# Feed-forward products of a cross-attention kernel as three fp32r matmuls on high and low parts

## The reference

```python
qn = layernorm(x, ln_q_g, ln_q_b);  q = qn @ Wq * scale
k, v = split(media @ Wkv)                            # 16 heads of 64
attn = softmax(where(mask, q k^T, -inf));  x = x + tanh(attn_gate) * (attn v) @ Wo
h = layernorm(x, ln_ff_g, ln_ff_b)
x = x + tanh(ff_gate) * gelu(h @ W1, exact) @ W2     # W1 256 x 1024, W2 1024 x 256
# second layer, on x:
mem = media @ W_mem^T;  ctx = softmax(x mem^T / 16) mem
gate = sigmoid([x, ctx] @ W_gate^T + b_gate);  out = rmsnorm(x + gate * ctx) * norm_w
```

## Time and profile before

| | us |
|---|---|
| median of 3 runs (lowest, highest) | 870.41 (870.37, 870.51) |
| profiled execution | 869.72 |
| span in its trace, first to last instruction | 867.9 |
| PE busy in the span | 831.4 |
| DVE, ACT, POOL busy | 591.0, 465.6, 401.2 |

### The profile page before, as it was taken

The page is one execution under the profiler, slowest core; times in us unless marked ns, Lnnn a source line. Parts: engine busy times, 40 slices in busy tenths (PEclk is TensorE's granted clock), DMA queues, the critical chain, the costliest instruction groups (busy, mean ns, idle before and its releaser), DMA issues.

```text
span 867.9 us, 18230 instructions
## 1 busy us (share of the span) xinstructions
PE 831.4 (96%) x7777; PEld 698.4 (80%) x7777; DVE 591.0 (68%) x968; ACT 465.6 (54%) x727; POOL 401.2 (46%) x189
## 2 busy tenths in 40 slices
PE   4999999999999999999999999999999999998986
PEld 3788888888888888888888888888888778887775
DVE  7856788867577888675688886756788622126375
ACT  5755666657356666573566665635555441226352
POOL 2445565655625656556256565553566650000002
PEclk9999999999999999999999999999999999999999
DMA  9100001000000010000000000000000700000201
GB/s 283 26 1 2 2 5 37 1 2 2 2 1 2 10 32 1 2 2 2 2 1 2 2 1 2 2 2 2 1 2 4 214 1 1 1 1 1 77 1 48
DMA packets 20559, 16.80 MB, mean 19 GB/s; under 512 B 1008, under 2 KB 19456, under 8 KB 20480
## 3 DMA queue, kind: packets, MB, share of 16 engines
q1 hardware_dynamic: 20192, 15.38, 6.0%
q10 hardware_dynamic: 288, 0.27, 0.1%
HBM read 14.59 MB, written 1.05 MB: 18 GB/s over the span
## 4 chain that ended last, share of the span: by engine, by line
PE 81%; DVE 11%; ACT 4%; POOL 2%; issue 1%; DMA 1%; ACTq 0%; POOLq 0%; DVEq 0%
PE psum L1284 21%; PE psum L1298 17%; PE psum L345 15%; PE psum L1253 6%; PE psum L1209 4%; PE psum L1313 3%; PE psum L1060 3%; PE psum L1074 3%; PE psum L1148 2%; DVE mx L901 2%; DVE ot L931 1%; DVE k_lo L890 1%; PE psum L1304 1%; ACT v L614 1%; POOL acc L450 1%
## 5 line engine op out<-in xcount | busy, mean ns | idle before, releaser
L450 POOL TENSOR_TENSOR acc<-acc,ring 128x1024 f32<-128x1024 f32 x128 | 306.8, 2397 | 18.7 <-POOL acc L445 0.5
L901 DVE TENSOR_REDUCE mx<-psum 128x2 f32<-128x800 f32 (+2 forms) x256 | 245.2, 989 | 84.5 <-PE psum L1253 72.4
L631 ACT ACTIVATE ring<-psum 128x1024 f32<-128x1024 f32 x192 | 197.0, 1027 | 65.7 <-PE psum L1284 59.2
L445 POOL TENSOR_TENSOR acc<-ring 128x1024 f32<-128x1024 f32 x32 | 77.0, 2405 | 271.6 <-ACT ring L631 271.6
L1298 PE MATMUL psum<-ring,v 128*64 128x256 f32 (+1 forms) x1664 | 186.7, 381 | 1.8
L1298 PEld LDWEIGHTS psum<-ring,v 128*64 128x64 f32 (+1 forms) x1664 | 116.7, 137 | 61.1 <-DVE k_lo L890 3.9
L1284 PE MATMUL psum<-nm,maskrow 64*128 64x256 f32 (+1 forms) x832 | 123.9, 294 | 0.6 <-ACT ring L631 0.6
L1284 PE MATMUL psum<-q_lo,k_hi 64*128 64x256 f32 (+1 forms) x832 | 116.9, 278 | 0.0
L1284 PE MATMUL psum<-q_hi,k_hi 64*128 64x256 f32 (+1 forms) x832 | 116.7, 277 | 0.0
L1284 PE MATMUL psum<-q_hi,k_lo 64*128 64x256 f32 (+1 forms) x832 | 116.5, 277 | 0.0
L623 ACT COPY od<-psum 128x512 f32<-128x512 f32 x32 | 18.8, 588 | 161.0 <-PE psum L1304 161.0
(11 more groups left out here) (150 smaller groups left out, 1352.9 us busy)
## 6 DMA issues: line engine op xcount, KB each, us to landing
nat<-in_ctx_dram SPq DMA_DIRECT2D x7, 768.0 KB
w<-in_L_xattn_W_dram SPq DMA_DIRECT2D x2, 1024.0 KB, 8.7
wo<-in_L_xattn_Wo_dram SPq DMA_DIRECT2D x1, 1024.0 KB, 9.7
out_dram<-t_res SPq DMA_DIRECT2D x8, 128.0 KB, 1.7
mask<-in_mask_BxS_bk_dram SPq DMA_DIRECT2D x4, 200.1 KB, 7.1
nat<-in_ctx_dram SPq DMA_DIRECT2D x2, 384.0 KB, 7.4
ring<-in_L_xattn_Wkv_dram SPq DMA_DIRECT2D x2, 384.0 KB, 6.2
wq<-in_L_xattn_Wq_dram SPq DMA_DIRECT2D x1, 768.0 KB, 6.7
```

What stands on the lines that cost most here:

```text
L445: nc.gpsimd.tensor_tensor(acc[:, :, :, :], ring[:, 0, :, :, :], ring[:, 1, :, :, :], ALU.add)\
L450: nc.gpsimd.tensor_tensor(acc[:, :, :, :], acc[:, :, :, :], ring[:, g, :, :, :], ALU.add)\
L631: nc.scalar.activation(ring[:, g, :, :, :], score_set[m % 2].rearrange("p (h i q) -> p h i q", h=2, i=2), ACT.Exp).then_inc(S["p_ready"], 1)
L901: nc.vector.tensor_reduce(mx[:, t, :, c], pair[:, :, 0:min(c1, KEYS) - c0], axis=AX.X, op=ALU.max).then_inc(S["m_max"], 1)
```

## The change

The feed-forward products get the form that the projections have. `hidden` and `ff_out` do three fp32r matmuls for each float32 one. Four things supply the parts:

- POOL splits W1 in four pieces of 128x512, two behind pair 3 and two behind pair 4 of the last batch (each a cast and a subtraction), and W2 likewise behind pairs 6 and 7 (`split_ff_weights`). It first waits for the DVE fold of that pair (`acc_ready`).
- DVE splits the tokens (`split_tokens`, item `d.i`, 128x512) and the GELU's result (`split_gelu`, item `e.i.half`, 128x1024), again a cast and a subtraction.
- `h.0.0` moves from ahead of `A.6` to behind the last scores `S.7.6`. In the calls behind the list, `ff_sum(0)` moves ahead of the copy of `wctx`, and the splits stand between.
- W1 is loaded earlier (when the fourth batch's tokens are projected, into the place of `mt` and `wq`), with a semaphore of its own, as has W2. The late tiles are laid out by hand at fixed offsets.

Waits for finished tokens become waits for split tokens (`ff_zt`), or for the unsplit ones (`ff_zfull`) where those are used; `ff_out` waits for the split GELU (`ff_gsplit`) and all eight pieces (`ff_w_split`).

```diff
-               ("R", 7): "w.0 h.0.0", ("S", 7, 6): "h.0.1 g.0.0 g.0.1", ("A", 7): "h.1.0",
-               ("D", 7): "z.2 g.1.0 h.1.1 g.1.1"}
+               ("U", 6): "d.0 d.1", ("R", 7): "w.0", ("S", 7, 6): "h.0.0 h.0.1 g.0.0 g.0.1", ("A", 7): "h.1.0 e.0.0 e.0.1",
+               ("D", 7): "z.2 g.1.0 h.1.1 g.1.1", ("F", 7): "d.2 e.1.0 e.1.1"}
...
-            upto(sp, "t_full", BATCH - 1, TUNITS)
+            upto(sp, "mt_lo", BATCH - 1, NCH)
             upto(sp, "g_full", BATCH - 1, PAIRS // 2)
+            sp.dma_start(w1[:, :, :], W1.rearrange("(t p) n -> p t n", p=P)).then_inc(S["w1_in"], 16)
             upto(sp, "k_full", BATCH - 1, PAIRS * NCH)
...
+            def split_ff_weights(n, pieces):
+                raw, hi, lo, landed = ((w1, w1_hi, w1_lo, "w1_in"), (w2, w2_hi, w2_lo, "w2_in"))[n]
+                pool.wait_ge(S[landed], 16)
+                for i in pieces:
+                    at_once = [t.rearrange("p a n -> p (a n)")[:, 512 * i:512 * (i + 1)] for t in (hi, raw, lo)]
+                    nc.gpsimd.tensor_copy(at_once[0], at_once[1]).then_inc(S["ff_w_hi"], 1)
+                    pool.wait_ge(S["ff_w_hi"], 4 * n + i + 1)
+                    nc.gpsimd.tensor_tensor(at_once[2], at_once[1], at_once[0].bitcast(F32), ALU.subtract)\
+                        .then_inc(S["ff_w_split"], 1)
+            FF_PIECES = {3: (0, (0, 1)), 4: (0, (2, 3)), 6: (1, (0, 1)), 7: (1, (2, 3))}
...
+                    if not next_batch and j in FF_PIECES:
+                        upto(pool, "acc_ready", b, j + 1)
+                        split_ff_weights(*FF_PIECES[j])
...
+            def split_tokens(i):
+                dve.wait_ge(S["ff_zfull"], i + 1)
+                tail_step(nc.vector.tensor_copy(zts_hi[i][:, :, :], zts[i][:, :, :]))
+                nc.vector.tensor_tensor(zts_lo[i][:, :, :], zts[i][:, :, :], zts_hi[i][:, :, :].bitcast(F32),
+                                        ALU.subtract).then_inc(S["ff_zt"], 1)
+            def split_gelu(i, half):
+                lane, f = i % LANES, slice(4 * half, 4 * half + 4)
+                dve.wait_ge(S["ff_gelu"], 2 * i + half + 1)
+                tail_step(nc.vector.tensor_copy(gts_hi[lane][:, f, :], gts[lane][:, f, :]))
+                nc.vector.tensor_tensor(gts_lo[lane][:, f, :], gts[lane][:, f, :], gts_hi[lane][:, f, :].bitcast(F32),
+                                        ALU.subtract).then_inc(S["ff_gsplit"], 1)
...
             normalised(BATCH - 1)
+            ff_sum(0)
+            split_gelu(2, 0)
             dve.wait_ge(S["wctx_psum"], 1)
             nc.vector.tensor_copy(wctx[:, :], wctx_psum).then_inc(S["wctx_ready"], 1)
-            ff_sum(0)
+            split_gelu(2, 1)
+            split_tokens(3)
             ff_sum(1)
+            split_gelu(3, 0)
             memory_lo(0)
+            split_gelu(3, 1)
             memory_lo(1)
...
-                    for t in range(DT):
-                        last = mm(dst[:, (f % 4) * TOK:(f % 4 + 1) * TOK], w1[:, t, f * P:(f + 1) * P],
-                                  zts[i][:, t, :], start=(t == 0), stop=(t == DT - 1))
+                    c = slice(f * P, (f + 1) * P)
+                    last = split_mm(dst[:, (f % 4) * TOK:(f % 4 + 1) * TOK],
+                                    [(w[:, t, c], z_t[i][:, t, :]) for t in range(DT)
+                                     for w, z_t in ((w1_hi, zts_hi), (w1_lo, zts_hi), (w1_hi, zts_lo))])
...
-                            pe.wait_ge(S["ff_gelu"], 2 * i + f // 4 + 1)
-                        last = mm(ff2_psum[i][:, t * DIM:(t + 1) * DIM], gts[i % LANES][:, f, t * P:(t + 1) * P],
-                                  w2[:, f, :], start=(f == 0), stop=(f == FT - 1))
+                            pe.wait_ge(S["ff_gsplit"], 2 * i + f // 4 + 1)
+                        for n, (g, w) in enumerate(((hi, w2_hi), (hi, w2_lo), (lo, w2_hi))):
+                            last = mm(ff2_psum[i][:, t * DIM:(t + 1) * DIM], g[:, f, q], w[:, f, :],
+                                      start=(f == 0 and n == 0), stop=(f == FT - 1 and n == 2))
```

More of the change, by code:

```diff
@@ L3 @@
 from contextlib import ExitStack
+import math
 F32 = mybir.dt.float32
@@ L178, in sb @@
             return ctx.enter_context(nc.sbuf_tensor(name, shape, dt))
+        starts, used = {}, [0]
         def ph(name, shape, dt=F32):
+            starts[name] = used[0]
+            used[0] += (mybir.dt.size(dt) * math.prod(shape[1:]) + 31) // 32 * 32
             return phase.enter_context(nc.sbuf_tensor(name, shape, dt))
@@ L230, in cross_attention_kernel @@
         phase.close()
[L234 to L242, removed]
-        nats = [nat0, nat1]
-        def lanes(name, shape, dt=F32):
-            return [ph(f"{name}{lane}", shape, dt) for lane in range(LANES)]
@@ L249, in cross_attention_kernel @@
[L249 to L267, removed]
+        def at(offset, name, shape, dt=F32):
+            with ExitStack() as spot:
+                if offset:
+                    spot.enter_context(nc.sbuf_tensor(f"below_{name}", [P, offset], U8))
+                return spot.enter_context(nc.sbuf_tensor(name, shape, dt))
@@ new lines, in spread @@
+        def spread(offset, name, shape, n, dt=F32):
+            size = (4 * math.prod(shape[1:]) + 31) // 32 * 32
+            return [at(offset + i * size, f"{name}{i}", shape, dt) for i in range(n)]
+        KB = 1024
+        MT_SIZE = 4 * KPAD + 24
+        MT_AT = 16 * KB + 2 * MT_SIZE
+        assert starts["mt"] == MT_AT
+        w2, w2_lo = at(0, "w2", [P, FT, DIM]), at(0, "w2_lo", [P, FT, DIM], F32R)
+        w2_hi = at(8 * KB, "w2_hi", [P, FT, DIM], F32R)
+        nat1 = at(16 * KB, "nat1", [P, KT, MED])
@@ new lines, in cross_attention_kernel @@
+        raw_wg = at(16 * KB + 4 * KT * MED, "raw_wg", [P, DT, 2 * DIM])
+        wm = at(20 * KB + 4 * KT * MED, "wm", [P, DT, MED])
+        bgate = at(21 * KB + 4 * KT * MED, "bgate", [P, DIM])
+        w1, w1_lo = at(MT_AT, "w1", [P, DT, FF]), at(MT_AT, "w1_lo", [P, DT, FF], F32R)
+        w1_hi = at(MT_AT + 8 * KB, "w1_hi", [P, DT, FF], F32R)
+        normw = at(MT_AT + 16 * KB, "normw", [P, DIM])
+        wctx = at(MT_AT + 17 * KB, "wctx", [MED, 2 * DIM])
+        nats = [nat0, nat1]
+        DEAD_Z, DEAD_UNREAD, DEAD_V, DEAD_K, DEAD_RING = [starts[t] for t in ("z", "unread", "v", "k_hi", "ring")]
@@ new lines, in cross_attention_kernel @@
+        wg = at(DEAD_V + 6 * KB, "wg", [P, 2 * DT, DIM])
+        gts, gts_lo = spread(DEAD_K, "t_gelu", [P, FT, TOK], LANES), spread(DEAD_K, "t_gelu_lo", [P, FT, TOK], LANES, F32R)
+        gts_hi = spread(DEAD_K + 16 * KB, "t_gelu_hi", [P, FT, TOK], LANES, F32R)
+        mts_hi = spread(DEAD_RING, "t_mt_hi", [MED, KPAD], LANES, F32R)
+        mts_lo = spread(DEAD_RING + LANES * MT_SIZE, "t_mt_lo", [MED, KPAD], LANES, F32R)
+        free = DEAD_RING + 2 * LANES * MT_SIZE
+        gms_hi, gms_lo = spread(free, "t_gm_hi", [MED, TOK], LANES, F32R), spread(free + 2 * KB, "t_gm_lo", [MED, TOK], LANES, F32R)
@@ new lines, in cross_attention_kernel @@
+        cxs, gxs, gate_s, fuseds, squares, ress = (
+            spread(free + 4 * KB * (i + 1), name, [P, QT, DIM], LANES)
+            for i, name in enumerate(("t_cx", "t_gx", "t_gate", "t_fused", "t_square", "t_res")))
+        uts = spread(free + 28 * KB, "t_u", [MED, TOK], LANES)
+        l1top, l1max, l1den, l1rec, l1sum = (
+            spread(free + 30 * KB + 64 * i, name, [P, QT], LANES)
+            for i, name in enumerate(("t_top", "t_max", "t_den", "t_rec", "t_sum")))
+        p1s = [at(0, "t_p10", [P, QT, KPAD]), at(MT_AT, "t_p11", [P, QT, KPAD])]
@@ L268, in cross_attention_kernel @@
+        pts = spread(DEAD_K, "t_pt", [P, KT, TOK], LANES)
         ctx.enter_context(phase)
@@ L490, in turned_in @@
                                                 ACT.Identity, scale=norms[:, 2, t:t + 1], bias=norms[:, 3, t:t + 1])
-                last.then_inc(S["ff_zt"], 1)
+                last.then_inc(S["ff_zfull"], 1)
             def gelu(i, half):
@@ L944, in attention @@
                         normalised(n)
+                    elif kind == "d":
+                        split_tokens(n)
+                    elif kind == "e":
+                        split_gelu(n, item[2])
                 assert steps[0] in (0, PER["attention_step"]), steps[0]
```

30 lines of the change are left out of this document (18 added, 12 removed).

## The result

| | before | after |
|---|---|---|
| median of 4 runs (lowest, highest), us | 870.39 (869.50, 870.51) | 861.18 (860.30, 861.67) |
| profiled execution, us | 869.72 | 861.04 |
| span in its trace, us | 867.9 | 859.2 |
| PE busy in the span, us | 831.4 | 822.5 |
| DVE, ACT, POOL busy, us | 591.0, 465.6, 401.2 | 615.8, 465.2, 419.3 |

The ratio is 0.9896, with a 95% interval of 0.9884 to 0.9908: 9.2 us faster in the medians, against the 861.4 us of the forecast.

A forecast was written before the change was run, and what follows sets the result against it. PE was taken as the bound, almost without a break from 724 us. Terms -10.0 + 1.65 - 0.34 - 0.7 gave -9.4, and 0.4 us of waiting at O made -9.0: 861.4 us as median, range 860.2 to 863.9.

The forecast's parts named there:

- Passes: Products by W1 and W2: 384 fp32r passes at 0.118 us replace 256 at 0.216, removing 10.0 us of PE.
- D.6: After A.6, PE waits for the fold of pair 6, so D.6 begins at 695.95: a new wait of 1.65 us.
- h.0.1 and turn_x2: PE's wait of 0.34 us ahead of h.0.1 goes; that ahead of the first turn_x2 falls from 1.13 to 0.45.
- Pieces on POOL: POOL's splits of W1 and W2: cast 0.61 and subtraction 1.28 us, 1.9 us a piece, 3.8 for two.
- Splits on DVE: DVE's splits: GELU half 1.9 us, tokens 1.1; cast of 1024 columns 0.69, subtraction 1.2 us.
- the rival with slow casts: DVE casts at the two-input rate, nothing hidden: O 3.1 us late, -6.3 us, 864.1; chance 0.08.
- the tight place: Second turned_memory needs memory_lo(0), queued behind split_gelu(3,0): 0.6 us to spare, 0.1 if DVE casts at 1.2.
- Where both meet: DVE and POOL take turns behind pairs 6 and 7, 0.14 us hidden at each of DVE's four; O waits 0.4 us.
- nothing hidden: Rival: turns of DVE and POOL hide nothing, PE waits 1.55 us ahead of O, -7.85 us, 862.6; chance 0.27.
- no collision: Rival: POOL's and DVE's instructions fall into each other's semaphore gaps, O doesn't wait, -9.4 us, 861.0; chance 0.13.
- The sum: Whole kernel: -9.0 us, 860.7 for a profiled execution, 861.4 as the median; chance 0.45.
- POOL as the bound: Rival: POOL's split instructions take 2.4 us each, O 12.1 us late, +2.7 us, 873.1; chance 0.03.

The follow-up runs named there:

- DVE's addition: Changed kernel with the last of pair 6's five additions done by DVE instead of POOL: 860.08 us, ratio 0.9879 to the kernel before.
- undoing the order: Changed kernel with the copy of wctx put back ahead of ff_sum(0) and the first half of batch 2's GELU split: 862.21 us.
- W2 alone: Changed kernel with the eight hidden float32 again and W1 and the tokens not split, order of calls kept: 866.41 us.
- the casts four times: Changed kernel with each of POOL's casts of W2 done four times: 866.43 us, beside 870.60 us of the kernel before.

## Why the prediction was right

**Passes.** Right in kind and count; the term was 10.0 us and came to about 9.7. A pass takes 0.1188 us, not 0.118: an `ff_out` lost 6.91 - 5.70 = 1.21 us instead of 1.25, a `hidden` 3.45 - 2.84 = 0.61 instead of 0.62. That is no sign of slower passes than the projections': the earlier trace rows span ten gaps (eleven starts, not ten) in steps of 0.01 us, so 0.118 was read to some 0.001 us, and 0.001 us on 384 passes is 0.4 us. What the array does within the two records of a float32 matmul no run shows; the sum needs only their 0.216 us.

**D.6.** Predicted at 695.95 in the time of before, bound by the fold; it started at 696.45 - 0.52 = 695.93, and so it did without any split. The wait that I put at 1.65 us shows as 1.36, because the trace counts it from the end of the last matmul of `A.6`, and `D.6` without a wait begins 0.16 us ahead of that end (before: at 697.85, where `A.6` ran from 692.18 for 5.83 us). From start to start, `A.6` to `D.6` took 5.67 us before and 7.20 now: the wait costs 1.53, and `A.6` itself began 0.1 us later than in my sum. DVE's addition, which took 1.17 us off the wait, brought the scores 1.2 us forward.

**h.0.1 and turn_x2.** The first wait is gone, the second is 0.44 where I had 0.45; undoing the order gave 1.13.

**Pieces on POOL.** Alone they take 0.61 and 1.29 us, as read off; behind pair 6 of the kernel with W2 alone DVE splits nothing beside them:

```profile
696.69 0.61 POOL L473 CAST w_hi<-w 128x512 fp32r<-128x512 f32 x1 [1.58 <-DVE acc L978]
697.38 1.29 POOL L475 TENSOR_TENSOR w_lo<-w,w_hi 128x512 fp32r<-128x512 f32 x1
```

Behind pairs 3 and 4 they cost at most 0.1 us: the traces stand 0.44 us apart at 600 us and 0.52 at the mark.

**Splits on DVE.** The cast of 1024 columns takes 0.69 us, the half rate that I took, the subtraction 1.23 (1.2 predicted); the rival with slow casts is out. At the tight place, the second `turned_memory`, `memory_lo(0)` ended at 756.37 and PE came at 756.96: the 0.6 us to spare that I had.

**Where both meet.** Here one term was mis-sized. I had 0.14 us hidden at each of DVE's instructions and none at POOL's. The rows show it at both: POOL's second cast behind pair 7 (from 718.53) ends 719.60, 0.46 us after DVE's cast at 719.14 where alone it takes 0.61; DVE's last subtraction ends 1.08 us after that cast, 1.23 alone; POOL's last 1.15 after DVE's, 1.29 alone. The ends follow one another as turns would have them, so nothing hidden and no collision are both out as accounts of these places. That is the blocking of the Trainium skill (SBUF — State Buffer, Who interferes with whom), under which whoever comes first keeps the shared ports for its whole instruction; the trace agrees, but for some 0.14 us that each side saves where it waits (that this is its start-up is my reading; no run takes it apart). So pair 7's sums started 4.9 instead of 5.45 us after the fold of pair 6, and `ot` was done at 722.58 + 0.42 - 0.52 = 722.5 in the time of before, not 723.3. `O` waited for nothing: it began 1.2 us earlier than before, where I had 0.8. That is what my rival without collisions said of `O`, but for another reason; the collisions are all there, and they ended in the room that PE's 24 passes of `h.1.1` leave.

**The sum.** Against the mark, `O` is 1.21 us earlier (0.8 predicted), the stretch from `O` to the scores is 56.43 - 48.45 = 7.98 us shorter (8.18 predicted), and from there on nothing differs (87.4 us in both): -9.2 against -9.0. The two misses, 0.4 of a wait that didn't come and 0.2 of cadence, have opposite signs, so that the total came this close is in part luck; and -9.2 lies as far from the -9.4 of the rival without collisions as from my -9.0, so only the rows of DVE and POOL tell these two apart. The profiled executions differ by 8.68 only, for the 0.52 us ahead of the mark.

**POOL as the bound.** It isn't, but there is little room. In my sum there was none: `O` already waits 0.4 us there, and the 2.0 us for each POOL instruction are where the whole gain is lost. My expectation for the casts four times, that the forecast leaves room for twice POOL's time, misread this. Measured, `od` is ready for the reciprocals at 720.73 and DVE's last split ends at 719.17 + 1.51 = 720.68; `ot` ends at 723.00, and with the 0.14 us from `ot` to `O` that the run with the casts four times shows, `O` could have begun 0.2 us sooner. With POOL's time behind pair 6 at 9.05 us (696.54 to 705.59 in that run) instead of 4.84, `O` waited 2.88 us. The splits that stand ahead of the reciprocals, not the sums of the next pair alone, carry POOL's time to PE.

## What to carry to other kernels

A product whose float32 matmuls show two passes in the trace can be three fp32r passes (low by low is left out) and be faster; what it gains can be summed beforehand if the pass cadence is read from the same shape in the same kernel. Here that was 0.119 against 0.216 us, and that term is the result: the moves around it cost 0.5 us. Work that was moved away from a place may have hidden a wait there; look what its neighbour then waits for, and shorten that (an addition given to an idle engine) rather than fill it. Where two engines hold each other up, as DVE and POOL do here, count turns, with what both save while they wait, and ask what queues behind the last of them.

## What was not expected of the hardware

- DVE beside POOL's sums: a cast of 0.42 us lasted 2.58 and a subtraction of 0.69 lasted 2.75, while POOL's sums kept their 9.97 us for four.
- Behind an idle PE of 2.88 us, ahead of `O`, the granted clock was 0.50 for some 3 us, and `O` took 1.5 us longer; behind idle stretches of 1.36 us (`D.6`) and 1.69 us (`ff_out(0)`) the windows show 1.00.
- DVE's reciprocals, 4 in 1.79 us, kept that time beside POOL's pieces (720.76, POOL busy until 721.83).
